# Four Gelu activations with a bias column, and the attention's addition on GpSimd

## The chip, the cores and the metric

The kernel runs on one core of one Trainium2 chip. Its time is the device time of that core in microseconds; three runs gave 814.64, 816.70 and 813.89 us, median 814.64. The profile is of one further execution.

## What is computed

A network of two layers on 16 sequences of 256 tokens with 128 channels (4096 tokens). Each layer adds to its input an attention-like part and a mixture of experts, both computed from the layer-normed input. In the first layer the attention-like part is a selective scan. In the second it is a product of softmaxes without a sequence dimension: for each token, Q, K and V are read as 16 heads of 8 channels, K is softmaxed over the heads and gives an 8x8 matrix with V, and the softmaxed Q is multiplied by it. The experts of the second layer:

```python
logits = xf @ Wg.T + bg
probs = softmax(logits); tp, ti = top_k(probs, 2); tp = tp / (sum(tp) + EPS_TOPK)
h = gelu(einsum('td,efd->tef', xf, W1) + b1)        # 8 experts, 512 hidden channels
y = einsum('tef,edf->ted', h, W2) + b2
x = x + attention + sum over the two experts of tp * y
```

Here b1 is one number per expert and hidden channel, so with hidden channels on partitions it is a column.

## The kernel before

One program, five instruction streams (SyncE, GpSimd, ScalarE, TensorE, VectorE) that are written out by hand, one block of code each, and synchronised by semaphores alone. Within an engine the order of the code is the order of execution; nothing reorders it.

The experts' work is laid out in 72 blocks of 128 token slots, sorted by expert. Both layers use the same block functions. In the second layer a loop of ticks runs them, 9 ticks to each of 8 groups of attention (`BPG`, `TICKS[1]`), and 7 more ticks to drain (`DRAIN`). Each engine has its own `blocks_tick`. At tick t:

- GpSimd (lines 491 to 509) fetches the rows of block t+4 by an indirect DMA (L496) and sends the results of block t-6 by another (L502). Its loop over the ticks is at lines 531 and 532.
- TensorE turns the rows of blocks t and t+1 if t is even (`block_turn`, L868), does the up projection of block t-2 (`block_up`) and the down projection of block t-4 (`block_down`, L899 for the second bias, L902 for four fp32 products). `block_up` first writes the first bias over a whole bank, as the product of `b1_parts` with the selection matrix `chosen`, 512 columns (L880). Then, for each of the four 128-channel chunks, three fp16 products of high and low parts are added (L886, L887, L888).
- ScalarE copies out the result of block t-5 (`block_out`, L661), copies the turned rows (`block_in`, L646, even t) and applies Gelu to block t-2, one activation of 128x512 from PSUM to `hid_f` (`block_gelu`, L654).

The number of a block's expert is in `eid`. TensorE reads it into a register (`experts_of`, L346) once per block and addresses weights and selections with it. ScalarE has no use of it.

Waits between these: the up projection of a block waits for the Gelu of two blocks before (two banks, `ph`), the Gelu for its up projection and for a free one of three buffers, the down projection for its Gelu and a free output bank, the output copy for the send that had its buffer four blocks before.

Between blocks, the attention of a group g runs: TensorE makes Q and K of group g+1 behind tick 2 of group g (`head_products`, L990) and V behind tick 6 (`head_values`, L998). ScalarE takes the two exponentials of group g+1 behind tick 7 (`head_exps`, L757), which needs another activation table than Gelu, so two table loads go with them. VectorE runs through `head_state`, `head_shift` of the next group, `head_turn` and `head_out`, with four operations on 4096 elements per partition (L1429, L1434, L1448, L1453), then scales the output `o_` (L1455) and adds it to x (L1456). After the loop SyncE loads the sent results group by group, ScalarE scales half of them (L558), VectorE combines them with x (`combine`, L1175 and L1180), and ScalarE's queue writes the output.

Of the kernel before, what the change touches and what calls it, by code (L numbers as in the profile page):

```python
# [21 lines left out]
P = 128  # L22
# [3 lines left out]
GROUPS = 8  # L26
# [20 lines left out]
QKV = 2  # L47
VALUES = 6
EXPS = 7
DRAIN = 7  # L50
# [36 lines left out]
def build(nc, a, out):  # L87
    ctx = ExitStack()
    with ctx:
# [6 lines left out]
        def sem(name):  # L96
            return ctx.enter_context(nc.semaphore(name))
# [131 lines left out]
        s_qkv, s_v = sem("s_qkv"), sem("s_v")  # L229
        s_qks, s_qke = sem("s_qks"), sem("s_qke")  # L230
        s_tran, s_wkv = sem("s_tran"), sem("s_wkv")
        block = ctx.enter_context(nc.Block())
# [15 lines left out]
        yT = work[:, 7, :]  # L248
        q_of = (work[:, 0, :], work[:, 7, :])
        work_all = work[:, :, :].rearrange("p a c -> p (a c)")  # L250
# [177 lines left out]
        def _(e):  # L428
# [45 lines left out]
            for l in range(2):  # L474
# [52 lines left out]
                if l == 1:  # L527
                    indices_in(1)
                    for b in range(AHEAD):
                        fetch(b)  # L530
                for tick in range(BLOCKS + DRAIN) if l else range(CLOSE, BLOCKS + DRAIN):
                    blocks_tick(tick)


        @block.scalar
        def _(e):
# [110 lines left out]

            def block_gelu(l, b):

                at = l * BLOCKS + b  # L650
                e.wait_ge(s_l1, at + 1)
                if at >= FR:
                    e.wait_ge(s_l2, at - FR + 1)
                e.activation(hid_f[:, b % FR, :], ph[:, b % 2, :], ACT.Gelu).then_inc(s_gelu, 1)  # L654

# [6 lines left out]

            def blocks_tick(l, tick):
                if l == 1 and (b := block_at(tick, DOWN + 1)) is not None:
                    block_out(l, b)
                if (b := block_at(tick, 0)) is not None and b % 2 == 0:
                    block_in(l, b)
                if (b := block_at(tick, 2)) is not None:
                    block_gelu(l, b)

# [88 lines left out]
            def head_group(g):  # L759
                for i, tick in enumerate(ticks_of(1, g)):  # L760
                    blocks_tick(1, tick)
                    if g + 1 < GROUPS:
                        if i == EXPS:
                            head_exps(g + 1)

            e.wait_ge(s_topw, 2)
            head_exps(0)
            for g in range(GROUPS):
                head_group(g)
            for tick in range(BLOCKS, BLOCKS + DRAIN):  # L770
                blocks_tick(1, tick)
            for g in range(GROUPS + 2):
# [10 lines left out]
        def _(e):  # L783
# [88 lines left out]
            def block_up(l, b, expert):  # L872

                at = l * BLOCKS + b
                en = expert(b)
                e.wait_ge(s_xrout, at // 2 + 1)
                if at >= 2:
                    e.wait_ge(s_gelu, at - 1)
                xh, xl = (xrT[:, b // 2 % 2, (b % 2 * 2 + k) * D:(b % 2 * 2 + k + 1) * D] for k in range(2))
                e.matmul(ph[:, b % 2, :].rearrange("p (c t) -> p c t", c=HC), b1_parts[:, :],  # L880
                         chosen[:, bass.ds(en * HC + l * NE * HC, HC)].unsqueeze(2).to_broadcast([P, HC, P]),
                         start=True, stop=False)
                for c in range(HC):
                    w = bass.ds(en * HID + (l * NE * HID + c * P), P)
                    o = ph[:, b % 2, c * P:(c + 1) * P]
                    e.matmul(o, w1h[:, w], xh, start=False, stop=False)  # L886
                    e.matmul(o, w1h[:, w], xl, start=False, stop=False)  # L887
                    ins = e.matmul(o, w1l[:, w], xh, start=False, stop=(c == HC - 1))  # L888
                ins.then_inc(s_l1, 1)
# [135 lines left out]
        def _(e):  # L1025
# [376 lines left out]

            k_, t_, o_ = (work[:, i, :] for i in (1, 3, 4))
            raw = t_[:, TG * HD * HD:2 * TG * HD * HD]
# [17 lines left out]
            def head_state(g):  # L1422

                e.wait_ge(s_qke, g * 2 + 2)
                e.wait_ge(s_v, g + 1)
                e.tensor_reduce(qsum, q_of[g % 2].rearrange("p (c d) -> p c d", d=HD), AX_X, ALU.add)
                st.seq(e.tensor_reduce(ksum, k_.rearrange("p (c h) -> p c h", h=HEADS), AX_X, ALU.add))
# [18 lines left out]
            def head_out(g):  # L1446
# [4 lines left out]
                                       turn.rearrange("p (t c) -> p t c", c=HD * HD).unsqueeze(2).to_broadcast(  # L1451
                                           [P, TG, HEADS, HD * HD]), ALU.mult))
                st.seq(e.tensor_reduce(o_, product[:, 1, :, :].rearrange("p t (x d) -> p (t x) d", d=HD), AX_X, ALU.add))  # L1453
                o3 = o_.rearrange("p (c d) -> p c d", d=HD)
                st.seq(e.tensor_tensor(o3, o3, qsum.unsqueeze(2).to_broadcast([P, TG * HEADS, HD]), ALU.mult))  # L1455
                e.tensor_tensor(x_all[:, group(g)], x_all[:, group(g)], o_, ALU.add).then_inc(s_att, 1)  # L1456

# [8 lines left out]
            for turn_ in range(0, GROUPS // BACK):  # L1466
                for q in range(BACK):
                    combine(1, turn_, q)

# [35 lines left out]
```

## Time and profile before

| | |
|---|---|
| median of 3 runs | 814.64 us (813.89 to 816.70) |
| the profiled execution's own time | 816.14 us |
| its span, first to last instruction | 814.4 us |
| mean granted TensorE clock | 0.854 |
| TensorE matmul busy | 590.9 us, 4512 instructions |
| VectorE busy | 680.0 us, 1242 |
| GpSimd busy | 512.7 us, 525 |
| ScalarE busy | 455.0 us, 825 |

The page gives busy time per engine and groups of instructions by line; a trace behind it can be asked for an engine's instructions in order of time, for the chain of work that ended last, and for waits. PE is TensorE's matmul, PEld its weight load, PEldq the sequencer in front of it, DVE VectorE, ACT ScalarE, POOL GpSimd, SP SyncE. A row of a timeline has the start, the duration, the engine, the line, the operation with output and input, and in brackets the idle time before it with what released it; "issue" there is idle time with no wait that the profile can show. Matmuls overlap in the array, so that the distance from one start to the next tells more than a duration. All rows are of one core, in microseconds from the start of the span.

### The profile page before, as it was taken

The page shows a single profiled execution, that of the slowest core. Times are in us where ns is not written, and L with a number is a line of the kernel's source. Part 1 is how long each engine was busy: PE and PEld are TensorE (multiplying, and loading weights), DVE is VectorE, ACT ScalarE, POOL GpSimd, SP SyncE. Part 2 cuts the span into 40 slices and gives each one's busy share as a digit, 9 for nine tenths or more (in the row PEclk, how much of TensorE's full clock was granted, in tenths as well). Part 3 has the DMA queues.
Part 4 walks back from the last instruction along what each step waited for, and adds up shares of the span by engine and source line. Part 5 has one row for each costly group of instructions (what it writes and reads, how often), then busy time and mean ns, then how long its engine had stood idle before and what let it go on. Part 6 is the DMA issues. An engine that isn't in the chain of part 4 may idle for free.

```text
span 814.4 us, 15691 instructions
## 1 busy us (share of the span) xinstructions
PE 590.9 (73%) x4512; PEld 429.4 (53%) x4512; DVE 680.0 (83%) x1242; ACT 455.0 (56%) x825; POOL 512.7 (63%) x525
## 2 busy tenths in 40 slices
PE   3774046669989889798989911913499999999960
PEld 2442012236666556566667601902488878888740
DVE  6886689998888787987977758797999999999907
ACT  1768189748776567647554234860255455554525
POOL 2443077779888888888898910135556776767530
PEclk9755559899999999999999955555599999999995
DMA  8521342345444444443444361020111111111119
GB/s 219 188 82 55 118 91 92 113 117 133 135 123 121 122 122 124 121 127 114 132 112 112 102 169 38 27 78 1 32 41 42 54 45 44 48 46 49 43 46 277
DMA packets 69211, 78.40 MB, mean 96 GB/s; under 512 B 10896, under 2 KB 44150, under 8 KB 69136
## 3 DMA queue, kind: packets, MB, share of 16 engines
q1 hardware_dynamic: 54320, 57.32, 24.8%
q0 software_dynamic: 9216, 17.85, 8.0%
q10 hardware_dynamic: 5600, 2.24, 1.0%
q8 instruction: 46, 0.75, 0.4%
q14 instruction: 29, 0.24, 0.1%
HBM read 62.43 MB, written 15.99 MB: 96 GB/s over the span
## 4 chain that ended last, share of the span: by engine, by line
PE 39%; DVE 25%; POOL 12%; issue 11%; ACT 9%; DMA 4%; SPq 0%; DVEq 0%; POOLq 0%; ACTq 0%
PE po L902 7%; DVE work L1282 7%; PE pb L902 4%; PE pb L857 4%; POOL work L516 4%; PE ph L886 4%; PE ph L880 4%; POOL results L502 3%; POOL xrow L496 3%; PE ph L888 3%; PE ph L887 3%; DVE pb L1272 2%; ACT decay L638 2%; POOL arena L299 2%; DVE work L1059 2%
## 5 line engine op out<-in xcount | busy, mean ns | idle before, releaser
L502 POOL DMA_INDIRECT results<-res,pair_of x144 | 150.7, 1047 | 67.8 <-issue 34.8
L496 POOL DMA_INDIRECT xrow<-rows,row_of x144 | 148.7, 1033 | 43.5 <-issue 25.9
L1282 DVE TENSOR_TENSOR_SCAN work<-decay,pb 128x512 f32<-128x512 f32 x128 | 154.7, 1208 | 11.2 <-PE pb L857 11.0
L654 ACT ACTIVATE arena<-ph 128x512 f32<-128x512 f32 x144 | 86.3, 599 | 121.1 <-PE ph L888 120.3
L902 PE MATMUL po<-w2f,arena 128*128 x864 | 123.2, 286 | 0.1
L857 PE MATMUL pb<-work,idf 128*128 128x512 f32 x214 | 116.3, 633 | 2.6 <-POOL work L516 1.4
L886 PE MATMUL ph<-xrT,w1h 128*128 128x128 f16 x576 | 114.3, 223 | 0.1
L888 PE MATMUL ph<-xrT,w1l 128*128 128x128 f16 x576 | 113.4, 220 | 0.0
L887 PE MATMUL ph<-xrT,w1h 128*128 128x128 f16 x576 | 113.1, 220 | 0.0
L902 PEld LDWEIGHTS po<-w2f,arena 128*128 128x128 f32 x864 | 105.2, 192 | 2.3 <-issue 0.6
L838 PE MATMUL pb<-parts,pick 128*128 128x512 bf16 x128 | 50.6, 405 | 56.0 <-DVE work L1282 46.6
L1272 DVE TENSOR_TENSOR pb<-work,pb 128x512 f32<-128x512 f32 x128 | 86.1, 679 | 1.9 <-PE pb L838 1.6
L638 ACT ACTIVATE decay<-big,avec 128x510 f32<-128x510 f32 x128 | 81.5, 708 | 5.5 <-DVE work L1282 5.3
L299 POOL TENSOR_SCALAR arena<-count_h,mask 128x72 bf16<-128x72 bf16 x88 | 53.9, 614 | 42.8 <-DVE eid L1154 27.3
L646 ACT COPY xrT<-px 128x512 f16<-128x512 f16 x72 | 42.2, 585 | 56.1 <-PE px L868 55.9
L886 PEld LDWEIGHTS ph<-xrT,w1h 128*128 x576 | 56.1, 97 | 19.8 <-issue 6.7
L516 POOL TENSOR_TENSOR work<-work,c_ring 128x512 f32<-128x512 f32 x49 | 62.9, 1302 | 3.4 <-DVE work L1282 3.2
L887 PEld LDWEIGHTS ph<-xrT,w1h 128*128 x576 | 56.9, 99 | 9.4 <-issue 0.3
L838 PEld LDWEIGHTS pb<-parts,pick 128*128 128x128 bf16 x128 | 12.6, 99 | 91.9 <-DVE work L1282 80.7
L880 PE MATMUL ph<-chosen,b_parts 128*128 x144 | 55.6, 386 | 7.2 <-issue 3.2
L516 POOL TENSOR_TENSOR work<-work 128x512 f32<-128x512 f32 x42 | 54.1, 1296 | 6.5 <-DVE work L1282 6.3
L888 PEld LDWEIGHTS ph<-xrT,w1l 128*128 x576 | 56.3, 98 | 0.8
(219 smaller groups left out, 1266.6 us busy)
## 6 DMA issues: line engine op xcount, KB each, us to landing
work<-c_rows SPq DMA_DIRECT2D x64, 256.0 KB
c_ring<-c_rows SPq DMA_DIRECT2D x64, 256.0 KB
decay<-in_w SPq DMA_DIRECT2D x16, 256.0 KB, 3.4
w2f<-in_w SPq DMA_DIRECT2D x8, 512.0 KB, 7.1
rows<-rows SPq DMA_DIRECT2D x16, 256.0 KB, 2.2
decay<-results SPq DMA_DIRECT2D x16, 256.0 KB, 4.2
big<-results SPq DMA_DIRECT2D x16, 256.0 KB, 4.9
xrow<-rows,row_of POOLq DMA_INDIRECT x144, 3.1
```

The source lines that it names most:

```text
L496: e.indirect_dma_start(xrow[:, b % XR, :], None, rows_dram[l], bass.IndirectOffsetOnAxis(row_of[:, b:b + 1], 0)).then_inc(s_row[b % XR], 16)
L502: e.indirect_dma_start(res_dram[l], bass.IndirectOffsetOnAxis(pair_of[:, b:b + 1], 0), res[:, b % RR, :], None, bounds_check=NRES - 1, oob ...
L516: e.tensor_tensor(product_row(at), product_row(at), c_row(at), ALU.mult).then_inc(s_prod, 1)
L638: e.activation(inner[0], inner[1], ACT.Exp, scale=avec[:, n:n + 1]).then_inc(s_a, 1)
L857: e.matmul(py, idf[:, :], product_row(g * NS + n), start=(n == 0), stop=(n == NS - 1))\
L880: e.matmul(ph[:, b % 2, :].rearrange("p (c t) -> p c t", c=HC), b1_parts[:, :], chosen[:, bass.ds(en * HC + l * NE * HC, HC)].unsqueeze(2) ...
L886: e.matmul(o, w1h[:, w], xh, start=False, stop=False)
L887: e.matmul(o, w1h[:, w], xl, start=False, stop=False)
L888: ins = e.matmul(o, w1l[:, w], xh, start=False, stop=(c == HC - 1))
L902: ins = e.matmul(o, hid_f[:, b % FR, c * P:(c + 1) * P], w2f[:, bass.ds(en * HID + (l * NE * HID + c * D), D)], start=False, stop=(c == HC ...
L1272: e.tensor_tensor(pb[:, at % 3, :], dx, pb[:, at % 3, :], ALU.mult).then_inc(s_bx, 1)
L1282: e.tensor_tensor_scan(product_row(at), decay[:, n, :], pb[:, at % 3, :], 0.0, ALU.mult, ALU.add).then_inc(s_scan, 1)
```

## The change

Two edits, both in the second layer's loop.

The first bias: TensorE's selection product (L880) is left out for the second layer, and the first product of each chunk starts its own accumulation. ScalarE reads the number of the block's expert into a register of its own and applies Gelu in four activations of 128x128, each with its chunk's column of b1 as bias. The first layer keeps its product and its one activation.

The addition: GpSimd adds the attention's output `o_` to x for groups 0 to 6, behind the block work of tick 4 of the next group; for the last group VectorE keeps it. VectorE waits for that addition before it writes `o_` again and before it combines; it signals GpSimd with `s_att` when the scaling is done.

```diff
+ADDED = 4
...
+        s_xatt = sem("s_xatt")
...
-        q_of = (work[:, 0, :], work[:, 7, :])
+        q_of, o_ = (work[:, 0, :], work[:, 7, :]), work[:, 4, :]
...
+                def add_heads(g):
+
+                    e.wait_ge(s_att, GROUPS + g + 2)
+                    e.tensor_tensor(x_all[:, group(g)], x_all[:, group(g)], o_, ALU.add).then_inc(s_xatt, 1)
+
                 for tick in range(BLOCKS + DRAIN) if l else range(CLOSE, BLOCKS + DRAIN):
                     blocks_tick(tick)
+                    if l == 1 and tick % BPG == ADDED and 0 < tick // BPG < GROUPS:
+                        add_heads(tick // BPG - 1)
...
-            def block_gelu(l, b):
+            def block_gelu(l, b, expert):
 
                 at = l * BLOCKS + b
+                en = expert(b) if l == 1 else None
                 e.wait_ge(s_l1, at + 1)
                 if at >= FR:
                     e.wait_ge(s_l2, at - FR + 1)
-                e.activation(hid_f[:, b % FR, :], ph[:, b % 2, :], ACT.Gelu).then_inc(s_gelu, 1)
+                if l == 1:
+                    for c in range(HC):
+                        ins = e.activation(hid_f[:, b % FR, c * P:(c + 1) * P], ph[:, b % 2, c * P:(c + 1) * P], ACT.Gelu,
+                                           bias=b1[:, col(en * HC + (NE * HC + c))])
+                else:
+                    ins = e.activation(hid_f[:, b % FR, :], ph[:, b % 2, :], ACT.Gelu)
+                ins.then_inc(s_gelu, 1)
...
             e.wait_ge(s_topw, 2)
+            expert = experts_of(e)
             head_exps(0)
...
-                e.matmul(ph[:, b % 2, :].rearrange("p (c t) -> p c t", c=HC), b1_parts[:, :],
-                         chosen[:, bass.ds(en * HC + l * NE * HC, HC)].unsqueeze(2).to_broadcast([P, HC, P]),
-                         start=True, stop=False)
+                if l == 0:
+                    e.matmul(ph[:, b % 2, :].rearrange("p (c t) -> p c t", c=HC), b1_parts[:, :],
+                             chosen[:, bass.ds(en * HC + l * NE * HC, HC)].unsqueeze(2).to_broadcast([P, HC, P]),
+                             start=True, stop=False)
...
-                    e.matmul(o, w1h[:, w], xh, start=False, stop=False)
+                    e.matmul(o, w1h[:, w], xh, start=(l == 1), stop=False)
                     e.matmul(o, w1h[:, w], xl, start=False, stop=False)
-                    ins = e.matmul(o, w1l[:, w], xh, start=False, stop=(c == HC - 1))
+                    ins = e.matmul(o, w1l[:, w], xh, start=False, stop=(l == 1 or c == HC - 1))
...
                 e.wait_ge(s_v, g + 1)
+                if g > 0:
+                    e.wait_ge(s_att, GROUPS + g + 1)
...
+                if g > 0:
+                    e.wait_ge(s_xatt, g)
                 st.seq(e.tensor_reduce(o_, product[:, 1, :, :].rearrange("p t (x d) -> p (t x) d", d=HD), AX_X, ALU.add))
                 o3 = o_.rearrange("p (c d) -> p c d", d=HD)
-                st.seq(e.tensor_tensor(o3, o3, qsum.unsqueeze(2).to_broadcast([P, TG * HEADS, HD]), ALU.mult))
-                e.tensor_tensor(x_all[:, group(g)], x_all[:, group(g)], o_, ALU.add).then_inc(s_att, 1)
+                e.tensor_tensor(o3, o3, qsum.unsqueeze(2).to_broadcast([P, TG * HEADS, HD]), ALU.mult).then_inc(s_att, 1)
+                if g == GROUPS - 1:
+                    e.wait_ge(s_att, 2 * GROUPS + 1)
+                    e.tensor_tensor(x_all[:, group(g)], x_all[:, group(g)], o_, ALU.add).then_inc(s_xatt, 1)
...
                 for q in range(BACK):
+                    e.wait_ge(s_xatt, turn_ * BACK + q + 1)
                     combine(1, turn_, q)
```

## Rows read from the trace of the kernel before

**Rows 1.** busy by stretch: length; PE, PEld, DVE, ACT, POOL; clock, DMA share, GB/s
```profile
...
661.00:712.00 51.00, 49.88 (x485) 42.16 (x484) 48.61 (x29) 27.23 (x54) 36.13 (x37) 1.00 0.15 45
...
```

**Rows 2.** chain that ended last (start us, us, what)
```profile
...
610.52 1.79 PE pb L990 x16
...
737.45 1.79 PE pb L990 x16
...
786.58 0.27 ACT res L661
...
786.91 0.97 POOL results L502
...
796.66 1.29 ACT big L558 x4
...
```

**Rows 3.** PE in order of time (start us, us, engine, line, operation)
```profile
...
612.37 0.38 PE L880 MATMUL ph<-chosen,b_parts 128*128 x1
612.58 0.22 PE L886 MATMUL ph<-xrT,w1h 128*128 128x128 f16 x1
...
614.26 0.38 PE L880 MATMUL ph<-chosen,b_parts 128*128 x1
...
627.99 0.39 PE L880 MATMUL ph<-chosen,b_parts 128*128 x1
...
630.74 0.39 PE L880 MATMUL ph<-chosen,b_parts 128*128 x1 [0.26 <-ACT arena L654]
...
633.54 0.39 PE L880 MATMUL ph<-chosen,b_parts 128*128 x1
...
```

**Rows 4.** PE's sequencer, lines 346 and 880 (ns: shortest/median/longest)
```profile
...
L346 PEldq TENSOR_LOAD <-eid x144: 296/301/495, 175.9 to 781.1; - x144
L346 PEldq FUSED_REGOPS  x144: 151/151/165, 176.4 to 781.4; - x144
...
L880 PEldq FUSED_REGOPS  x144: 46/56/65, 176.7 to 781.8; - x144
...
```

**Rows 5.** GpSimd in order of time, after one group's exponentials
```profile
...
628.30 1.01 POOL L502 DMA_INDIRECT results<-res,pair_of  x1 [2.56 <-ACT res L661]
629.62 0.96 POOL L496 DMA_INDIRECT xrow<-rows,row_of  x1 [0.30 <-ACT res L661]
630.89 1.02 POOL L502 DMA_INDIRECT results<-res,pair_of  x1 [0.30 <-ACT res L661]
...
```

**Rows 6.** waits from 586 to 786 us (total us, times, longest us)
```profile
...
DVE work L1426 <- ACT work L757: 3.6, 5, 1.3
...
```

**Rows 7.** VectorE in order of time, second layer
```profile
...
774.86 0.69 DVE L1456 TENSOR_TENSOR x<-x,work 128x512 f32<-128x512 f32 x1
...
```

**Rows 8.** ACT's groups of instructions by line (busy us, mean ns)
```profile
...
L646 ACT COPY xrT<-px 128x512 f16<-128x512 f16 x72 | 42.2, 585 | 56.1 <-PE px L868 55.9
...
L558 ACT ACTIVATE big<-big,topw 128x128 f32<-128x128 f32 x32 | 10.2, 390 | 13.6 <-DMA big<-results 13.6
...
L661 ACT COPY res<-po 128x128 f32<-128x128 f32 x36 | 9.5, 263 | 16.8 <-PE po L902 16.7
...
```

**Rows 9.** ACT in order of time, around one group's exponentials
```profile
...
624.29 0.60 ACT L654 ACTIVATE arena<-ph 128x512 f32<-128x512 f32 x1 [0.30 <-PE ph L888]
624.90 1.28 ACT L757 ACT_TABLE_LOAD   x1
...
628.81 0.60 ACT L654 ACTIVATE arena<-ph 128x512 f32<-128x512 f32 x1
...
```

**Rows 10.** GpSimd in order of time, first layer
```profile
...
273.82 1.32 POOL L516 TENSOR_TENSOR work<-work 128x512 f32<-128x512 f32 x1
275.30 1.27 POOL L496 DMA_INDIRECT xrow<-rows,row_of  x1 [0.16 <-issue]
...
```

**Rows 11.** VectorE and GpSimd in order of time, first layer, around 308 us
```profile
...
308.28 2.04 DVE L1289 TENSOR_TENSOR work<-work 128x512 f32<-128x512 f32 x1
...
308.45 1.31 POOL L516 TENSOR_TENSOR work<-work 128x512 f32<-128x512 f32 x1
...
```

More of the change, by code:

```diff
@@ L661, in block_out, with blocks_tick @@
                 e.copy(res[:, b % RR, :], po_of(l, b)).then_inc(s_res, 1)
-            def blocks_tick(l, tick):
+            def blocks_tick(l, tick, expert=None):
                 if l == 1 and (b := block_at(tick, DOWN + 1)) is not None:
@@ L668, in blocks_tick @@
                 if (b := block_at(tick, 2)) is not None:
-                    block_gelu(l, b)
+                    block_gelu(l, b, expert)
             def lows(c):
@@ L760, in head_group @@
                 for i, tick in enumerate(ticks_of(1, g)):
-                    blocks_tick(1, tick)
+                    blocks_tick(1, tick, expert)
                     if g + 1 < GROUPS:
@@ L770, in _ @@
             for tick in range(BLOCKS, BLOCKS + DRAIN):
-                blocks_tick(1, tick)
+                blocks_tick(1, tick, expert)
             for g in range(GROUPS + 2):
@@ L1400, in _ @@
             rows_at(1)
-            k_, t_, o_ = (work[:, i, :] for i in (1, 3, 4))
+            k_, t_ = (work[:, i, :] for i in (1, 3))
             raw = t_[:, TG * HD * HD:2 * TG * HD * HD]
```

## The prediction, made before the changed kernel ran

> **What bounds the kernel now.** I read the table by stretches first, to see who is busy in the second layer's loop (about 580 to 788 us). In it TensorE, VectorE and GpSimd all look nearly full: in a stretch of 51 us PE is busy 49.9, DVE 48.6, POOL 36.1 and ACT 27.2, with a granted clock of 1.00, its upper level of 2.4 GHz [rows 1]. Then the chain that ended last: through the loop it lies on PE, leaves by ACT's copy of the last block at 786.58, GpSimd's last send at 786.91 and its landing, and a tail of loads and combines follows that this change hardly touches. The projections of one group follow each other by (737.45 - 610.52) / 5 = 25.39 us [rows 2]. That is the beat of the loop: 9 blocks and one set of projections.
>
> What holds PE to it? Two kinds of block stand in PE's timeline. From one bias product to the next takes 2.75 or 2.80 us in an ordinary block, but 1.89 us right after a group's projections, with the same instructions but for a turn of rows in every second block [rows 3]. In the ordinary one the array is idle in small pieces, because PE's sequencer is late: it reads the expert's number (0.30 us), works it up (0.15) and forms an address for each use (the bias product's takes 0.056) [rows 4]. So PE is bound mostly by its sequencer, not by its columns.
>
> Two engines are close behind. GpSimd sends and fetches once per block, two sends 2.59 us apart when it is not held up: 9 x 2.59 = 23.3 us of 25.39, and its one long pause, 2.56 us, stands where ACT does the exponentials [rows 5]. VectorE waits five times for ACT's exponentials, 3.6 us in all, and ends its last attention group at 774.86 + 0.69 = 775.6 us, 11 us before ACT's last copy [rows 2, 6, 7].
>
> **What the change takes from PE.** One bias product per block goes, 72 in all. In a block paced by the array it is worth the 0.21 us from its start to the next matmul's [rows 3]. In one paced by the sequencer it is worth the address, 0.056, and the dispatch of two instructions; for these I take 0.06, an estimate between nothing and the 0.15 that remains if the array's figure were the whole (0.21 - 0.056). So 0.12 us. Below it lies 0.056, above it the product's own recorded duration, 0.39 [rows 3, 4]. About three blocks in nine go at the array's pace: 3 x 0.21 + 6 x 0.12 = 1.35 us per group, 10.8 us for eight. The bounds are 72 x 0.056 = 4 and 72 x 0.39 = 28 us. The expert's number is still read on PE, since the weights are addressed by it; that stays.
>
> **What it adds to ACT.** One activation of 128x512 (0.60 us) becomes four of 128x128 with a bias column. The nearest row is ACT's scaling of results, 128x128 with a scale column: 0.39 us alone, four in 1.29 us [rows 2, 8]. So each block costs 1.29 - 0.60 = 0.69 us more, 50 us over the loop. Its bounds: four copies from PSUM without a column, 4 x 0.26 = 1.05 us, and four that don't overlap, 4 x 0.39 = 1.56 us. In front of them ACT now reads the expert's number as PE does: 0.30 + 0.15 us and gaps, about 0.6 us with the gaps, which are my estimate [rows 4]. It stands behind the copies in ACT's program, so the copy of the transposed rows (0.58 us, every second block) hides it; behind the output copy alone (0.26) some 0.35 us is open [rows 8]. One block then costs ACT 0.26 + 0.29 + 0.17 + 1.29 = 2.0 us, nine 18.1, and with two table loads and two exponentials (from 624.90 to 628.81, less one copy: 3.7 us) 21.8 of 25.39 [rows 9]. ACT is no longer idle but not the bound.
>
> **Where ACT does touch the path.** At the exponentials ACT leaves PE alone for 3.7 us: a Gelu at 624.29, the next at 628.81 to 629.41. The up projection two blocks later starts at 630.74, and although the profile puts down a wait of 0.26 us there, this block comes 2.75 us after the one before it and the next comes after 2.80, so I read it as the usual gap of the sequencer [rows 3, 9]. The cover is thus 630.74 - 629.41 = 1.33 us. After the change both Gelus are 0.69 longer and the number's reading adds 0.35, 1.73 us; PE itself arrives about 0.36 earlier, three blocks at 0.12. Stall: 1.73 + 0.36 - 1.33, about 0.8 us, seven times: 5.6 us. Bounds: 0 (with copies' prices) and 1.7 (no cover).
>
> **The moved addition.** On VectorE 0.69 us per group goes, and for the last group it stays. I cost this at nothing: the loop's end is not VectorE's, which has 11 us to spare, and between groups it waits for ACT's exponentials [rows 6, 7]. On GpSimd come seven additions of 128x512, in each group's block 4, between a send and a fetch. In the first layer such an addition takes 1.32 us there and the fetch behind it starts 0.16 later, where it is 0.30 without one [rows 5, 10]: 1.18 us net. Bounds: 1.18, and 1.32 + 0.16 + 0.30 (a fetch stretched from 0.97 to 1.27, as in that row) = 1.5 or so. GpSimd's group becomes 23.3 + 1.2 = 24.5 us. Queued behind the addition are a fetch, wanted by PE four blocks later, and a send; what it waits for, VectorE's scaling of the group before, was done more than a block earlier. VectorE's second big reduction now waits for the addition; it can come 1 to 3 us late if GpSimd lags, which VectorE's pause can hold in part, and its phase shifts once rather than each time.
>
> One rule speaks against the move. The row: a VectorE addition of 128x512 with both inputs in SBUF took 2.04 us while a GpSimd addition ran beside it; the same shape takes 0.69 undisturbed [rows 7, 11]. The Trainium skill (SBUF — State Buffer, the section on SBUF's two separate sides) says that GpSimd and a VectorE operation with two SBUF inputs exclude each other for the whole instruction. By that rule one collision per group would cost VectorE 1.3 us, 9 us in all, which its spare time would hold; the sum by rule and by row is the same unless GpSimd is the one that waits, which is part of the second rival.
>
> **The sum.** PE's group: 25.39 - 1.35 + 0.8 = 24.8 us, GpSimd's 24.5, VectorE's about 23.7: PE still leads by little. 10.8 gained and 5.6 given back leave 5.2 us. The profiled execution took 816.14 us (span 814.40 and 1.74 around it): 810.9. That execution lies 1.5 us above the median of 814.64, so the forecast for the median is 809.4 us. Its own range is 806 to 812.
>
> **Rivals.**
> 1. More of it arrives (chance 0.20). If the stall at the exponentials is covered (Gelu pieces near the copies' price) and the sequencer was the whole of PE's bound, PE gains 10.8 us or more; then GpSimd's floor decides: 25.39 - 24.5 = 0.9 us in seven groups, 6.3, and some 0.2 in each of the last 17 steps, 3.4: 9.7 us. 805 us. For it: the idle pieces in ordinary blocks. Against: ACT's late Gelus.
> 2. GpSimd takes it (0.17). If each addition costs 1.5 us and waits besides for a VectorE operation of 0.69, its group is 23.3 + 2.2 = 25.5, the beat of now, and only the last 17 steps gain 2 us: 812.6 us, no change that counts. For it: its 0.30 gaps in an unbroken row. Against: the big operations of VectorE in this stretch read one input from PSUM.
> 3. ACT becomes the bound, and the kernel slower (0.18). If the reading of the expert's number can't run beside the copy in front, it costs 0.6 in each block; with Gelu pieces 0.33 apart a block takes 0.26 + 0.29 + 0.6 + 1.32 = 2.47, a group 9 x 2.47 + 3.7 = 25.9. With stalls of the other engines around the exponentials, where nothing of it is hidden, I set 26.2: 0.8 x 7 = 5.7 us more, 820 us. The point from which it decides is a block of (25.39 - 3.7) / 9 = 2.41 us on ACT. For it: 50 us of new work and 72 readings on one queue. Against: the unbroken four in 1.29 us.
> 4. The change might do less than it says, if the sequencer merely waits elsewhere. That is inside the forecast's lower half, 812 us, and gets no chance of its own.
>
> **Chances.** Forecast 0.45, rivals 0.20, 0.17 and 0.18. About 0.3% (2.4 us) is what a measurement of this kernel can tell. Faster by more: nearly all of the first two, less the forecast's edge, plus a little of GpSimd's case: 0.61. Slower by more: 0.17. Between: 0.22. The range takes in rival 1 down to 802 (PE's bound above 0.12 and a cheaper addition) and leaves out the upper part of rival 3: 802 to 818.
>
> **What would show it.** Right: in ordinary blocks PE goes from 2.80 to about 2.68 us, and to 1.68 after projections; the projections' beat falls to 24.8; ACT's four pieces take 1.2 to 1.3 us; a new wait of PE for ACT's Gelu of about 0.8 us, seven times; GpSimd's pauses at the exponentials shrink from 2.5 to about 1.5. Wrong: a gap in front of most Gelus with PE long done (rival 3); no pause left on GpSimd and PE waiting for fetched rows (rival 2); ordinary blocks at 2.5 us or less (rival 1).

## The result and the profile after

The changed kernel takes 808.47 us (median of 4 runs, 807.37 to 809.08) beside 815.46 us before (4 runs): a ratio of 0.9916 with an interval of 0.9900 to 0.9931. That is 7.0 us less, where 5.2 were forecast; 808.47 lies inside the range of 802 to 818 and inside the likeliest case's own range of 806 to 812.

| | before | after |
|---|---|---|
| median | 815.46 us | 808.47 us |
| the profiled execution, its span | 816.14, 814.4 us | 808.11, 806.3 us |
| beat of the projections in the loop | 25.39 us | 24.50 us |
| last output copy of ACT starts | 786.58 us | 779.34 us |
| ACT busy, instructions | 455.0 us, 825 | 490.6 us, 1041 |
| TensorE matmul busy | 590.9 us | 568.4 us |
| mean granted clock | 0.854 | 0.857 |

The table by stretches of the kernel after, with the columns of [rows 1] (length, PE, PEld, DVE, ACT, POOL, granted clock, DMA share, GB/s):

```profile
...
661.00:712.00 51.00, 48.79 (x488) 41.13 (x486) 49.94 (x29) 37.53 (x113) 39.70 (x41) 1.00 0.16 47
...
```

PE has become a little less busy, ACT went from 27.2 to 37.5, GpSimd from 36.1 to 39.7. VectorE gave an addition away and its busy time still rises, from 48.6 to 49.9: its groups follow each other faster, and it loses time that the part on the shared interface tells of. The chain of the kernel after has the same marks as [rows 2], the projections of a group and ACT's last copy:

```profile
...
609.72 1.79 PE pb L1008 x16
...
732.24 1.79 PE pb L1008 x16
...
779.34 0.28 ACT res L677
...
```

(732.24 - 609.72) / 5 = 24.50 us, 0.89 less than before. Of the 8.0 us between the two profiled executions, 0.8 were there at the first of these marks, 4.4 came in these five groups, 2.0 from the last one to ACT's last copy, and 0.8 behind it, in the tail of loads, where the change does nothing.

PE in order of time, kernel after; the first product of each block stands where the bias product stood in [rows 3]:

```profile
...
611.57 0.22 PE L904 MATMUL ph<-xrT,w1h 128*128 128x128 f16 x1
...
613.28 0.23 PE L904 MATMUL ph<-xrT,w1h 128*128 128x128 f16 x1
...
615.96 0.23 PE L904 MATMUL ph<-xrT,w1h 128*128 128x128 f16 x1
...
626.35 0.23 PE L904 MATMUL ph<-xrT,w1h 128*128 128x128 f16 x1
...
629.22 0.23 PE L904 MATMUL ph<-xrT,w1h 128*128 128x128 f16 x1 [0.51 <-ACT arena L666]
...
```

The block behind the projections takes 1.71 us (1.89 before), an ordinary one 2.68 (2.80), and between 626.35 and 629.22 stands something new: 2.87 us, of which 0.51 is idle time that a Gelu ends. ACT over the same exponentials, to be laid beside [rows 9]:

```profile
...
622.74 1.15 ACT L666 ACTIVATE arena<-ph,b 128x128 f32<-128x128 f32 x4 [0.20 <-PE ph L906]
623.90 1.28 ACT L773 ACT_TABLE_LOAD   x1
625.20 1.15 ACT L773 ACTIVATE work<-work 128x512 f32<-128x512 f32 x2
626.25 0.25 ACT L677 COPY res<-po 128x128 f32<-128x128 f32 x1
626.52 1.28 ACT L666 ACT_TABLE_LOAD   x1
627.81 1.14 ACT L666 ACTIVATE arena<-ph,b 128x128 f32<-128x128 f32 x4
...
```

Four Gelus take 1.15 us where one took 0.60. From the output copy to the table load there is no gap beyond the usual, so the reading of the expert's number is not seen here, though ACT's sequencer does it 72 times, 0.28 us for the load and 0.15 for the register work:

```profile
...
L348 ACTq TENSOR_LOAD <-eid x72: 273/278/472, 583.0 to 774.8; - x72
L348 ACTq FUSED_REGOPS  x72: 152/152/173, 583.5 to 775.1; - x72
...
```

GpSimd with one of its seven additions, kernel after, against [rows 5, 10]:

```profile
...
639.15 1.31 POOL L536 TENSOR_TENSOR x<-x,work 128x512 f32<-128x512 f32 x1
640.62 0.99 POOL L498 DMA_INDIRECT xrow<-rows,row_of  x1 [0.16 <-issue]
...
762.17 1.31 POOL L536 TENSOR_TENSOR x<-x,work 128x512 f32<-128x512 f32 x1
...
```

From the second addition to the seventh there are (762.17 - 639.15) / 5 = 24.60 us: between them GpSimd has no pause left and is, by 0.1 us, slower than PE's beat. The waits of the loop and what follows it (580 to 790 us) are, in the kernel after, those below; GpSimd's 15.5 us stand before 606 us and behind 767. Before, GpSimd waited 29.7 us for ACT's results and PE 0.3 for a Gelu:

```profile
...
POOL results L504 <- ACT res L677: 15.5, 14, 3.5
...
PE ph L904 <- ACT arena L666: 4.6, 9, 0.7
DVE work L1446 <- ACT work L773: 0.8, 2, 0.5
...
```

### The profile page after: what moved, and what is told of

The parts are those of the page before. It is cut to its first block, busy times and chain, and to the rows that moved or that the text cites. A ratio compares the mean times of both kernels' runs of the same rounds, so it can differ in the third digit from the quotient of the medians.

```text
span 806.3 us, 16164 instructions
## 1 busy us (share of the span) xinstructions
PE 568.4 (71%) x4401; PEld 417.7 (52%) x4440; DVE 676.6 (84%) x1235; ACT 490.6 (61%) x1041; POOL 523.6 (65%) x532
## 4 chain that ended last, share of the span: by engine, by line
PE 31%; DVE 27%; issue 13%; ACT 12%; POOL 12%; DMA 4%; ACTq 1%; SPq 0%; DVEq 0%; POOLq 0%
DVE work L1300 7%; PE po L920 6%; PE ph L904 4%; POOL work L518 4%; PE pb L874 4%; POOL results L504 3%; PE pb L920 3%; DVE pb L1290 3%; POOL xrow L498 3%; PE ph L906 2%; PE ph L905 2%; ACT arena L666 2%; ACT decay L647 2%; PE pb L1008 2%; POOL arena L301 2%
## 5 line engine op out<-in xcount | busy, mean ns | idle before, releaser
L874 PE MATMUL pb<-work,idf 128*128 128x512 f32 x214 | 114.2, 623 | 15.4 <-DVE work L1300 10.6
L904 PE MATMUL ph<-xrT,w1h 128*128 128x128 f16 x576 | 117.4, 224 | 8.5 <-ACT arena L666 4.6
L905 PE MATMUL ph<-xrT,w1h 128*128 128x128 f16 x576 | 115.3, 221 | 0.0
L906 PE MATMUL ph<-xrT,w1l 128*128 128x128 f16 x576 | 115.3, 220 | 0.0
L666 ACT ACTIVATE arena<-ph,b 128x128 f32<-128x128 f32 x288 | 83.4, 384 | 43.4 <-PE ph L906 43.1
L669 ACT ACTIVATE arena<-ph 128x512 f32<-128x512 f32 x72 | 43.1, 599 | 66.7 <-PE ph L906 66.1
L855 PE MATMUL pb<-parts,pick 128*128 128x512 bf16 x89 | 35.2, 404 | 48.8 <-DVE work L1300 38.6
```

Of the source, the lines that this page charges most:

```text
L666: ins = e.activation(hid_f[:, b % FR, c * P:(c + 1) * P], ph[:, b % 2, c * P:(c + 1) * P], ACT.Gelu, bias=b1[:, col(en * HC + (NE * HC + c))])
L874: e.matmul(py, idf[:, :], product_row(g * NS + n), start=(n == 0), stop=(n == NS - 1))\
L904: e.matmul(o, w1h[:, w], xh, start=(l == 1), stop=False)
L906: ins = e.matmul(o, w1l[:, w], xh, start=False, stop=(l == 1 or c == HC - 1))
```

## The experiments

Twelve kernels ran. The first four shared a chip on which the kernel before took 815.7 us; it is called the first chip here, and the pair of the result, whose chip is not on record, is read with it since its kernel before took 815.46 us. The eight others ran, four and four, on two more chips on which that same kernel took 850.15 and 849.15 us. Where a run is read against one of another set, the text says so. The ratios are those on record; a quotient of the medians differs from them by about 0.2% at most.

**The bias alone.** The changed kernel with the addition put back on VectorE:

```diff
-                if g > 0:
-                    e.wait_ge(s_xatt, g)
...
-                e.tensor_tensor(o3, o3, ..., ALU.mult).then_inc(s_att, 1)
+                st.seq(e.tensor_tensor(o3, o3, ..., ALU.mult))
+                e.tensor_tensor(x_all[:, group(g)], x_all[:, group(g)], o_, ALU.add).then_inc(s_att, 1)
```

> The bias by four Gelus with a column alone; the addition stays on VectorE. Theory (the gain comes from TensorE's sequencer, and GpSimd's addition is neither needed nor felt): the projections' beat stays at 24.5 us, and the kernel takes the time of the changed one, 808.5 us within 1. VectorE's own work per group, 24.35 us, still fits under 24.5. Rival (VectorE would become the bound without the move): a beat above 24.6, VectorE without a wait for the exponentials, and 809.5 to 811 us. Second rival (GpSimd's addition costs the changed kernel something): this one is faster, 807 us or less, with pauses of GpSimd back at the exponentials.

808.89 us (5 runs), ratio 0.9913 (0.9899 to 0.9926) to the kernel before: the whole gain is here. The beat, from its chain, is (731.50 - 608.87) / 5 = 24.53 us. VectorE in order of time, the first operation of two successive groups:

```profile
...
626.28 0.68 DVE L1437 TENSOR_REDUCE work<-work 128x64 f32<-128x512 f32 x1
...
650.64 0.68 DVE L1437 TENSOR_REDUCE work<-work 128x64 f32<-128x512 f32 x1
...
```

They are 24.36 us apart, with no idle time in front of either: VectorE no longer waits for the exponentials, and is only 0.17 us per group short of being the bound. So the theory holds, by a narrow margin; the first rival was nearly right about VectorE. The second rival, that the addition costs the changed kernel something, falls.

**The addition alone.** The bias back as a product of TensorE, one Gelu:

```diff
-                if l == 0:
-                    e.matmul(ph[:, b % 2, :]..., b1_parts[:, :], chosen[...]..., start=True, stop=False)
+                e.matmul(ph[:, b % 2, :]..., b1_parts[:, :], chosen[...]..., start=True, stop=False)
```

> The addition on GpSimd alone; the bias stays a product of TensorE. Theory: TensorE's beat of 25.4 us is longer than VectorE's 23.7 and GpSimd's 24.6, so nothing moves: 815 us within 1, GpSimd's pauses shorter by 1.2 us per group. Rival (VectorE's 0.7 us per group is on the path in the groups where it doesn't wait for ACT): 812 to 813 us. Rival on the other side: GpSimd's additions delay fetches, 817 us or more, with TensorE waiting for rows.

815.79 us (11 runs), ratio 0.9999 (0.9990 to 1.0008). Nothing moves, as the theory had it. Its waits show where the 0.7 us per group went; before, VectorE waited 3.6 us for ACT in the loop:

```profile
...
POOL results L504 <- ACT res L671: 21.7, 19, 3.4
...
DVE work L1439 <- ACT work L767: 9.6, 6, 2.0
...
```

VectorE waits 6.0 us more for the exponentials than before (the additions taken from it are 7 x 0.69 = 4.8 of them), and GpSimd 8.0 us less for results (its new work is 7 x 1.17 = 8.2). The move trades pauses of the two.

**No bias, one Gelu.** What the product's removal is worth when ACT pays nothing; the second layer's first bias is left out, and with it ACT's reading of the number (`en = expert(b)`):

```diff
-                if l == 1:
-                    for c in range(HC):
-                        ins = e.activation(..., ACT.Gelu, bias=b1[:, col(en * HC + (NE * HC + c))])
-                else:
-                    ins = e.activation(hid_f[:, b % FR, :], ph[:, b % 2, :], ACT.Gelu)
+                ins = e.activation(hid_f[:, b % FR, :], ph[:, b % 2, :], ACT.Gelu)
```

> The changed kernel with one Gelu of 128x512 and no reading of the expert's number on ScalarE: the second layer's first bias is left out altogether. It shows what the product's removal is worth without what it costs on ScalarE. Theory: TensorE's nine waits for Gelu (4.6 us together) go, of which GpSimd gives back some, since its 24.6 us per group then bounds: beat 24.4 to 24.6, 806 to 808 us. Rival (those waits are the whole difference and GpSimd has room): 804 us, beat 24.0. Rival (they were hidden anyway): 808.5.

804.38 us (4 runs), ratio 0.9861 (0.9846 to 0.9876). The chain:

```profile
...
609.65 1.79 PE pb L1002 x16
...
729.86 1.79 PE pb L1002 x16
...
```

The beat is (729.86 - 609.65) / 5 = 24.04 us and the wait for Gelu is gone from PE's list, so the rival that gave GpSimd room wins. GpSimd's additions still follow each other every (761.41 - 638.49) / 5 = 24.58 us:

```profile
...
638.49 1.32 POOL L536 TENSOR_TENSOR x<-x,work 128x512 f32<-128x512 f32 x1
...
761.41 1.31 POOL L536 TENSOR_TENSOR x<-x,work 128x512 f32<-128x512 f32 x1
...
```

It falls 0.54 us behind per group and PE does not feel it, because a fetch is made four blocks ahead. That reserve can be read off: the fetch at 599.14 us stands 12.1 us ahead of PE's turn of the same rows at 611.28, the last fetch only 4.7 us ahead of its turn:

```profile
...
759.11 0.97 POOL L498 DMA_INDIRECT xrow<-rows,row_of  x1 [0.30 <-ACT res L671]
...
763.80 0.39 PE L879 MATMUL px<-idh,xrow 128*128 128x128 f16 x4
...
```

From issue to landing a fetch takes 3.1 us here (median, 2.4 to 5.4), so the loop ends with less than 2 us of reserve left: 7.4 us of it are used up. Being slower than the beat is not the same as being the bound, as long as the loop is short enough.

**Four Gelus, fixed column.** Without the reading of the expert's number on ACT; every block takes the column of expert 0:

```diff
-                en = expert(b) if l == 1 else None
...
-                                           bias=b1[:, col(en * HC + (NE * HC + c))])
+                                           bias=b1[:, col(NE * HC + c)])
```

> The changed kernel with four Gelus, but ScalarE doesn't read the expert's number: every block takes the bias column of expert 0. Theory (the reading runs beside ScalarE's copies and is hidden, save behind the exponentials): 808 us, the wait of TensorE for Gelu behind the exponentials shorter by 0.3 us or less. Rival (the reading is open time on ScalarE, 0.45 us a block): the waits for Gelu fall from 4.6 us to under 2 and the time to 806 or less.

807.26 us (4 runs), ratio 0.9900 (0.9884 to 0.9915). The waits of PE:

```profile
...
PE ph L903 <- ACT arena L665: 3.6, 8, 0.6
...
```

The wait falls from 4.6 to 3.6 us. The time lies 1.2 us under that of the changed kernel, but that one is of another set and the intervals of the two ratios overlap (0.9900 to 0.9931 there), so only the wait is clear of the noise. The theory named the right size and the wrong place. ACT's excursion to the exponentials, from the end of one Gelu to the start of the next, takes 3.92 or 4.41 us with the reading and without it: there it is hidden entirely. What is open stands in front of nearly every ordinary Gelu. Last product and Gelu of one block, the changed kernel:

```profile
...
619.31 0.22 PE L906 MATMUL ph<-xrT,w1l 128*128 128x128 f16 x1
619.68 1.15 ACT L666 ACTIVATE arena<-ph,b 128x128 f32<-128x128 f32 x4 [1.04 <-PE ph L906]
...
```

and with the fixed column:

```profile
...
619.19 0.22 PE L905 MATMUL ph<-xrT,w1l 128*128 128x128 f16 x1
619.45 1.14 ACT L665 ACTIVATE arena<-ph,b 128x128 f32<-128x128 f32 x4 [0.91 <-PE ph L905]
...
```

The Gelu starts 0.37 us behind the last product's start with the number from a register and 0.26 us with a fixed column. These 0.11 us are felt only where PE waits for a Gelu, behind the exponentials: the seven blocks there are 0.11 to 0.19 us shorter with the fixed column. Which part of the register addressing costs them (ACT's sequencer forms each column's address in 0.046 us) was not tested. Of the 4 us or so between the changed kernel and the one with no bias, then, some 1 us belongs to the number from a register and 3 us to the longer Gelus.

**More additions on GpSimd, an earlier place for the exponentials, an unchecked number: first set on a slower chip.** On one chip the kernel before took 850.15 us (17 runs). The edits, each against the changed kernel:

```diff
# one more addition, two more additions (range(1), range(2))
                     e.wait_ge(s_att, GROUPS + g + 2)
+                    for k in range(1):
+                        e.tensor_tensor(c_ring[:, k, :], work[:, 2, :], o_, ALU.add)
# exponentials a tick earlier
-EXPS = 7
+EXPS = 6
# number unchecked
-                    values[b] = e.value_load(eid[0:1, col(b)], min_val=0, max_val=NE - 1)
+                    values[b] = nc.values_load(eid[0:1, col(b)], engines=[e.engine], min_val=0, max_val=NE - 1,
+                                               skip_runtime_bounds_check_because="...")
```

> The changed kernel with one more GpSimd addition of the same shape beside each of the seven, into a tile that nobody reads. GpSimd's group becomes 24.6 + 1.3 = 25.9 us against TensorE's 24.5. Theory (GpSimd may fall behind by some blocks before a fetch comes late, and catches up when the fetches end): it falls 1.4 us further behind per group, about 9 us in all, of which most is held; 808.5 to 811 us. Rival (GpSimd is the bound already): 7 x 1.3 = 9 us more, 817.

> As before, with two more additions: 27.2 us per group on GpSimd. Theory: 2.7 us behind per group; the room of some 9 us is used up after three or four groups, then TensorE waits for fetched rows or ScalarE for sends, and the beat goes to GpSimd's: 816 to 819 us. Rival (GpSimd is the bound already): 826.

> The changed kernel with EXPS = 6: the exponentials stand behind the Gelu of tick 6, so that TensorE's value projections (0.9 us) and its next block run beside them. Theory (the wait behind the exponentials is real time on TensorE's path): TensorE's waits for Gelu fall from 4.6 us to under 1.5, the beat from 24.5 to about 24.1, 805 us, that is 3 to 4 us under the changed kernel. Rival (GpSimd's 24.6 per group holds the beat): 808. Rival (VectorE now gets its shifted Q and K too late, and its exponentials then): 809 or more.

> The changed kernel with the expert's number read without the check of its bounds, on TensorE and ScalarE (the number is clamped where it is made), so that the register work of 0.15 us and the check of 0.02 go from each reading. Theory (TensorE's sequencer is the bound in ordinary blocks): an ordinary block falls from 2.65 to about 2.45 us, TensorE's group to about 23, and the loop is then held by VectorE (23.7) and GpSimd (24.6, less what it may lag): beat 23.8 to 24.2, 803 to 806 us. Rival (the array or the waits for ScalarE bound it): ordinary blocks stay at 2.6 us, 808.

They took 862.24, 877.58, 862.18 and 852.57 us. All four are slower than the kernel before on that chip (ratios 1.0122, 1.0303, 1.0120 and 1.0035), so none of the times expected came, and what each edit does to the changed kernel can't be read from them, since that kernel was not beside them. The second set has it.

**The second set, with the changed kernel.**

> The changed kernel itself, beside the three below. On a chip where the kernel before takes 815 us: 808.5. On the chip of the last four runs the kernel before took 850 us, and TensorE's sequencer came late in the second layer's loop with pauses of up to 2 us between matmuls. If that is so here as well, the theory (what is lost there is TensorE's supply of instructions, so that it has no room left for ScalarE's longer Gelus) gives a changed kernel no faster than before, 850 to 862 us; the rival (the change gains 7 us there too) gives 843.

> EXPS = 6 as in the run on the slower chip, to be read against the changed kernel on the same chip. Theory (the wait behind the exponentials is real time): 3 to 4 us under the changed kernel, 805 us where that takes 808.5, TensorE's waits for Gelu under 1.5 us together. Rival (GpSimd's 24.6 us per group hold the beat): the same time as the changed kernel.

> EXPS = 6, and the expert's number read without the check of its bounds, on both engines. Theory (TensorE's sequencer bounds the ordinary block): ordinary blocks at 2.45 us instead of 2.65, TensorE's group under 23 us; then VectorE's 23.7 and GpSimd's 24.6 hold the loop: beat 24.0 to 24.4, only 0 to 2 us under EXPS = 6 alone, 803 to 805 us, with GpSimd without a pause and TensorE or ScalarE waiting for it. Rival (GpSimd's lag is never felt): 800 us or less. Rival (the array bounds the block): no change of the ordinary block.

> The changed kernel with two more additions of 128x512 on GpSimd per group, once more. GpSimd's group is 24.6 + 2.6 = 27.2 us. Theory (GpSimd may lag by some 9 us before it is felt, and then sets the beat): the first groups at TensorE's 24.5, the later at 27, 8 to 11 us over the changed kernel. Rival (GpSimd is the bound already): 18 us over it, every beat at 27. Rival (it is never felt): 0 to 2 us.

It met a third chip that behaves as the second: before 849.15 us (19 runs). The changed kernel took 856.89 us (10 runs), ratio 1.0075 (1.0047 to 1.0103), that is slower by 6 to 8 us; EXPS = 6 took 859.67, EXPS = 6 with the unchecked number 853.54 and the two more additions 877.88. So the same change is a gain in one set and a loss in another. Each chip was met in one set and at one time only, so that the chip and the time can't be told apart as the cause; "chip" below stands for both.

What differs between the changed kernel there and on the first chip is found in one place. The loop's first up projection starts at 583.91 us there and at 583.31 here, the last at 824.41 and 774.92: (824.41 - 583.91) - (774.92 - 583.31) = 48.9 of the 50.0 us between the two spans lie between them. In the loop PE's timeline has pauses inside one and the same block or projection. The changed kernel there, rows of PEld:

```profile
...
617.21 0.10 PEld L906 LDWEIGHTS ph<-xrT,w1l 128*128 x1 [1.02 <-issue]
618.63 0.10 PEld L905 LDWEIGHTS ph<-xrT,w1h 128*128 x1 [1.30 <-issue]
...
629.43 0.75 PEld L1016 LDWEIGHTS pb<-wkv,xT 128*128 128x128 f32 x6 [1.03 <-issue]
...
```

None of these waits for data: inputs, bank and buffer are those of the load before. Leaving out the loads that stand behind a Gelu, this loop has 25 pauses of 0.6 to 1.4 us, 22.9 us together, and on the first chip it has none. They come in clusters, 45 to 214 weight loads apart. That looks like a supply of instructions that comes late, but the traces don't show it: the instruction queue moved the same 45 packets of 0.74 MB in both. It stays a reading.

Two more losses come with the pauses. PE's granted clock falls to its lower level behind them (a product of 0.22 us at 617.24 takes 0.31 at 621.21) and rises again, eleven times in this loop. From 600 to 770 us the mean is 1.00 on the first chip and 0.93 on this one, with a fifth fewer matmuls done; first the first chip, then this one, with the columns of [rows 1]:

```profile
...
600.00:770.00 170.00, 161.68 (x1586) 134.87 (x1583) 166.40 (x89) 125.44 (x376) 130.35 (x129) 1.00 0.16 47
...
```

```profile
...
600.00:770.00 170.00, 140.52 (x1259) 117.91 (x1257) 132.80 (x72) 99.75 (x298) 104.46 (x103) 0.93 0.13 38
...
```

And the wait behind the exponentials, which the change brought, is larger: in the seven blocks there PE is idle for 4.3 us in all on the first chip and for 9.7 us on this one, as here, where the Gelu ends 0.27 us before:

```profile
...
671.12 0.23 PE L904 MATMUL ph<-xrT,w1h 128*128 128x128 f16 x1 [1.46 <-ACT arena L666]
...
```

That points at why a change that gains on one chip loses on another, but no trace of the kernel before was taken here, so it is not shown. The expectation for this run had the size (850 to 862 us) and excluded its rival, 843; its theory, no room left for ACT's longer Gelus, fits the larger wait and is not shown by more than that. The other engines wait as well; the waits of the loop (580 to 845 us):

```profile
...
POOL results L504 <- ACT res L677: 62.5, 29, 5.9
...
PE ph L906 <- issue: 3.9, 4, 1.9
...
```

What the eight kernels still tell:

- GpSimd's additions. Two more of them cost 877.88 - 856.89 = 21.0 us for 7 x 2.6 = 18 us of work. The theory had 8 to 11 us and its first rival 18, both with GpSimd setting a beat of 27 us. Neither is what the trace shows: GpSimd's additions are 35.3 us apart in most groups where its work is 27.2, and it waits 69.0 us for ACT's results (580 to 865 us). What has grown are PE's pauses: 51 of 0.6 to 1.4 us, 47.5 us together instead of 22.9, with a mean clock of 0.88 from 600 to 770 us. In the list of waits, the third product of each chunk, which never stands first in a block:

```profile
...
POOL results L504 <- ACT res L679: 69.0, 24, 6.8
...
PE ph L908 <- issue: 9.3, 13, 1.1
...
```

  Why more work on GpSimd goes with more pauses on PE was not tested. One more addition costs about 5 us (862.24 against 856.89, but on different chips). How much GpSimd may lag on the first chip was not measured beyond the 7.4 us above.
- The exponentials a tick earlier. 859.67 against 856.89, inside the scatter of its five runs (853.09 to 860.70). PE's waits for Gelu in the loop are 5.7 us instead of 7.0, where under 1.5 was expected: the waits did not go. Whether it removes them on a chip like the first stays open.
- The unchecked number. The check and its register work are gone from both sequencers; line 348 now has nothing but the load. TensorE's:

```profile
...
L348 PEldq TENSOR_LOAD <-eid x144: 295/301/494, 176.4 to 820.6; - x144
...
```

In the last blocks of the loop, where no attention is left and no pause falls, two kernels of the second set can be compared that differ in this alone. First the exponentials a tick earlier, PE in order of time:

```profile
...
814.42 0.23 PE L904 MATMUL ph<-xrT,w1h 128*128 128x128 f16 x1
...
816.98 0.23 PE L904 MATMUL ph<-xrT,w1h 128*128 128x128 f16 x1
...
819.50 0.23 PE L904 MATMUL ph<-xrT,w1h 128*128 128x128 f16 x1
...
```

Then the same blocks with the unchecked number as well:

```profile
...
816.96 0.22 PE L905 MATMUL ph<-xrT,w1h 128*128 128x128 f16 x1
...
819.24 0.23 PE L905 MATMUL ph<-xrT,w1h 128*128 128x128 f16 x1
...
821.50 0.23 PE L905 MATMUL ph<-xrT,w1h 128*128 128x128 f16 x1
...
```

The blocks take 2.56 and 2.52 us against 2.28 and 2.26, at the upper clock in both. That is the sequencer as the bound, shown by taking 0.17 us of its work away; 2.45 was expected and rather more than the 0.17 comes back, for which no run gives the reason. In the time of the whole it gives 853.54 (850.81 to 856.14, 10 runs) against 859.67, about 6 us where 0 to 2 were expected.

## Why the prediction was right

**The product on PE.** Forecast: 0.12 us in an ordinary block, 0.21 in one at the array's pace, 10.8 us together. Measured by leaving the bias out altogether (no bias, one Gelu; its moved addition is worth nothing by itself): 815.70 - 804.38 = 11.3 us, and in its trace the 71 distances from block to block are 0.149 us shorter on average than before, where 10.8 us in 72 blocks is 0.150. In the last eight blocks of the loop PE goes from (781.93 - 760.12) / 8 = 2.73 us to (774.92 - 754.16) / 8 = 2.60, so 0.13; behind the projections from 1.89 to 1.71. The reading of [rows 3, 4] held: in ordinary blocks the sequencer is late, and the recorded 0.39 us of the product would have promised 28 us.

**ACT's new work.** Forecast 0.69 us more per block; it was 1.15 - 0.60 = 0.55. The neighbour was four activations with a scale column from SBUF, 1.29 us; from PSUM and with a bias column a piece follows the last in about 0.26, where the neighbour's follow in 0.30. The step held, its size was a quarter too high.

**The number on ACT.** Forecast: hidden beside ACT's copies except for 0.35 us behind the exponentials. Behind the exponentials nothing of it is open; 0.11 us in front of each Gelu is, which the forecast did not have. At the stall it counts once, so the term was 0.24 too high.

**The stall behind the exponentials.** Forecast 0.8 us, seven times, 5.6 us. Measured block by block against the kernel with no bias, the seven are 0.33 to 0.66 us longer, 0.52 on average; as waits of PE 4.6 us in nine places; as time 4.1 to 4.5 us. The mechanism held and the mean is near, but the terms under it are off in both directions, and part of the nearness is luck. Too high were the two Gelus (by 2 x 0.14), the number (0.24) and PE's early arrival (0.36; with no bias its first product comes on average 0.19 us sooner behind the Gelu's end than before). Two things were left out on the other side. First, PE does not start when the Gelu ends: in all seven stalls its first product comes 0.26 us behind the Gelu's end, so of a cover of 1.33 us only 1.07 can be used. Second, the one group that was read is of the better of two kinds. In every second group a copy of turned rows falls into ACT's excursion, which then lasts 4.41 us instead of 3.92, and the cover is 655.91 - 654.87 = 1.04 us (kernel before, the Gelu ends at 654.87):

```profile
...
654.28 0.60 ACT L654 ACTIVATE arena<-ph 128x512 f32<-128x512 f32 x1
...
655.91 0.39 PE L880 MATMUL ph<-chosen,b_parts 128*128 x1
...
```

The stalls after differ accordingly: 0.60 to 0.66 us in these four groups, 0.33 to 0.41 in the three others. Put together, 0.8 - 0.28 - 0.24 - 0.16 + 0.26 + 4 / 7 x 0.27 comes to about 0.5. Of the miss of 1.8 us (7.0 measured, 5.2 forecast), 0.5 is the product and the rest this term.

**The addition.** Costed at nothing, and the two runs with one edit each bear it out: 0.9999 for the addition alone, 0.9913 for the bias alone against 0.9916 for both. Its price on GpSimd, 1.18 us net, shows as 1.31 + 0.16 against a gap of 0.30: 1.17. What I did not see is how near VectorE stood: with the bias alone it runs unbroken at 24.36 us under a beat of 24.53. Whether the move would pay once PE gains 0.2 us more per group was not run, and the next paragraph speaks against it.

**The interface that VectorE and GpSimd share.** It was weighed as a cost of up to 1.3 us per collision and as no change in the sum. In the kernel after, one VectorE operation of 128x256 (L1461, the first of `head_turn`) meets five of GpSimd's seven additions. Undisturbed it takes 0.43 us; in these groups 0.72, 1.14, 1.00, 1.14 and 1.12 us, and each time it ends 0.3 us behind the addition:

```profile
...
663.77 1.30 POOL L536 TENSOR_TENSOR x<-x,work 128x512 f32<-128x512 f32 x1
...
664.24 1.14 DVE L1461 TENSOR_TENSOR pb<-work 128x256 f32<-128x256 f32 x1
...
```

Both of its inputs are in SBUF (`raw` and the sums). VectorE's operations with one input in PSUM that meet the same additions keep their 0.68 or 0.69 us. The trace agrees with the rule of the Trainium skill (SBUF — State Buffer, on SBUF's two separate sides) that the two exclude each other. The same section of the Trainium skill gives the interface to whichever of the two starts first, and there the measurement differs: in [rows 11] VectorE starts 0.17 us ahead of GpSimd, and it is still VectorE that takes 2.04 us instead of 0.69, while GpSimd takes 1.31. GpSimd's seven additions in the loop take 1.30 to 1.31 us as well, so the case in which GpSimd waits, a part of the second rival, did not occur. The loss is 3.0 us in all, and from the third group on 0.56 to 0.71 us each: as much as the 0.69 us that the move takes from VectorE. VectorE, which should have come down to about 23.7 us per group, lies at 24.5 to 24.6 in the later groups, with 0.1 us of idle time in front of its first operation, and the move relieves neither engine. The time does not show it, since the beat is 24.5 either way.

**The rivals.** ACT as the bound was excluded by its own trace: it still idles up to 2.6 us in front of a Gelu. GpSimd taking the gain did not happen on the first chip, though its pauses vanished as that rival needs; its lag is carried by the fetches made ahead. On the third chip, the only slower one where the changed kernel itself ran, the sign was that of rival 3, but its mechanism is not shown: PE's pauses come first there, and none of the cases of the prediction had them. So the prediction is right for a chip on which the kernel before takes 815 us; that the pair was measured on such a chip is luck, since the prediction has no term for the pauses.

## What to carry over

Where a fast engine runs many small instructions with addresses from registers, price a removed one by its start-to-start distances in both kinds of block (array late, sequencer late), not by its recorded duration; here 0.15 us on average against 0.39. An engine with spare time on average still gives back part of a gain where it makes a long excursion (here two table loads and two exponentials): add its new work up over that excursion and compare it with the cover that the consumer had, less the time from the producer's end to the consumer's start (0.26 us here), and in every kind of group. And when a gain is below 1%, measure it on more than one chip: the same change was 0.8% faster on one and 0.75% slower on another.

## What the runs showed that was not expected

- The kernel before took 815 us on one chip and 849 to 850 us on two others. For the changed kernel nearly all of the difference lies in the second layer's loop, with 25 pauses of 0.6 to 1.4 us inside PE's blocks, a clock that falls behind them and longer waits behind the exponentials. The change is 0.8% faster on the one and 0.75% slower on one of the others. No trace of the kernel before was taken there, so which of its waits grew with the change is not shown.
- GpSimd's work, 0.54 us per group slower than the beat, cost nothing over seven groups on the first chip, while on a slower chip two more additions cost 21.0 us for 18 us of work, with GpSimd still waiting and PE's pauses doubled.
- An addition moved from VectorE to GpSimd took as much from VectorE again, 0.56 to 0.71 us, where it met one VectorE operation with both inputs in SBUF.
- Activations of 128x128 from PSUM with a bias column followed each other every 0.26 us, about 0.04 closer than those from SBUF with a scale column.
